# Two layer norms of the first tiles done by GpSimd in place of VectorE, in a fused attention and recurrent gate kernel

## Chip, cores and metric

One core of one Trainium2 chip. The metric is the device time of one execution in microseconds (us); lower is better.

## The reference

x is 8 x 512 x 512 (batch, position, feature), ctx_1024 of the same shape gives both keys and values.

```python
x = x + xattn(layernorm(x), ctx_1024, ctx_1024, W_proj, b_proj)
x = x + ffn(layernorm(x), ...)
```

`xattn` is attention with 16 heads of 32 features, in which a query sees the keys at most 64 positions away, then a projection with W_proj. `ffn` scans over the 8 batch entries with a 512 x 512 state c: ft and it are sigmoids and gt a tanh of xt @ w.T + c @ u.T + b, and c = ft * c + it * gt. The output is tanh(x @ wo.T + c_final @ uo.T + bo). The layer norm subtracts the mean of a row and multiplies by 1 / sqrt(var + 1e-5).

## The kernel before

The 4096 rows of x are 32 tiles of 128 rows; a tile has 4 slots, one for each group of 4 heads. A single list, `steps` (L114 to L330), holds all work in order, as pairs (kind, index). Each engine's program walks this same list and takes from it the kinds that are its own; so each engine works strictly in the list's order, and semaphores join the engines. n is the slot, i = n // 4 the tile, s = n % 4. The loop at L165 writes the list. Up to slot 19 ("early") a tile i does, in order: in s = 0 the projection ("proj", L806) of tile i-1, the copy of inverse sums ("recip", GpSimd L668), the query norm ("ln1b") of tile i+1, a pair of weight remainders ("rest", GpSimd L653), and the bias add ("bias", GpSimd L648) of tile i+1; in s = 1 the residual add ("resid", VectorE L1063) and the statistics ("stat2", with GpSimd's power at L673) of tile i-1, another "rest", the second norm ("ln2b", L1083) of tile i-1, and TensorE's transpose of the normed query rows ("query", L709); in s = 2 "turn2", TensorE's transpose of the second norm's output (L821), with ScalarE's rounding of it (L931) and VectorE's remainder (L1099), and in tiles 2 and 3 a third "rest"; in s = 3 the first statistics ("ln1", with GpSimd's power at L639) of tile i+2 and TensorE's "spread" of the inverse sums (L797), which waits for GpSimd's "recip". Each slot also has a "score" (L731, TensorE, then L1013, VectorE), "exp" (L901, ScalarE), "turn" (L743, L753) and "value" (L767, L774).

The pairs of L653 are spread by SPLIT_AT (L158): two in tile 1, three in tile 2, three in tile 3, two in tile 4. From slot 20 on the gates' matrix products ("cell", L684 to L686) fill TensorE between these steps, the projection follows the query norm in the list, and the pieces of attn_hi and attn_lo (L663) are made for it. SENT is 9 and TURNED_X 11: the query norm is a step of tiles 0 to 10 alone (later tiles load x already transposed and norm it in "query_norm"), while the second norm is a step of all 32 tiles.

One buffer, tile_row, holds in turn the normed query rows (xn), the attention output (attn) and the second norm's output (x2). So the query norm of tile i+1 waits for the projection of tile i-1, which reads attn (`projected`, up to tile 6), and for tiles 7 to 10 for the split of attn (`attn_split`, L663). The moments mv1 and mv2 and the inverse deviations rs1 and rs2 have two places each, used in turn. These are the lines of VectorE that normalise:

```python
dve.tensor_scalar(xn[:, :], xr[:, i % XR, :], mv1[:, r, 0:1], rs1[:, r:r + 1],
                  ALU.subtract, ALU.mult).then_inc(ln1, 1)
dve.tensor_scalar(x2[:, :], xr[:, i % XR, :], mv2[:, r, 0:1], rs2[:, r:r + 1],
                  ALU.subtract, ALU.mult).then_inc(x2_done, 1)
```

Of the kernel before, what the change touches and what calls it, by code (L numbers as in the profile page):

```python
# [7 lines left out]
ALU = mybir.AluOpType  # L8
# [12 lines left out]
def bass_xattn_ffn(nc, x, x_t, ctx_rows, ctx_t, w_proj, b_proj, w_gates, u_gates, biases, w_out, u_out, b_out, in_c,  # L21
# [41 lines left out]
    WHOLE = OWN_BANKS // G  # L63
# [3 lines left out]
    SENT = 2 * TT + 1  # L67
# [3 lines left out]
    TURNED_X = SENT + 2  # L71
    XR = 4
# [2 lines left out]


    MOVED = [j for j in range(SENT - 1, TILES) if j % TT < TT - 1]

    def moved(n):
        return sum(j < n for j in MOVED)  # L80

# [4 lines left out]
    def by_tensor(n):  # L86
        return n - moved(n)
# [77 lines left out]
    while cells_done < len(products):  # L165
        i, s = n // G, n % G
# [178 lines left out]
    with ExitStack() as ctx:  # L345
# [23 lines left out]
        xr = sb("xr", [P, XR, D], F32)  # L369
# [3 lines left out]
        xn = x2 = tile_row  # L373
# [26 lines left out]
        mv1 = invsum[:, MEAN:MEAN + 4].rearrange("p (r m) -> p r m", r=2)  # L400
        ve1, rs1 = invsum[:, MEAN + 4:MEAN + 6], invsum[:, RSTD:RSTD + 2]
# [11 lines left out]
        mv2 = moments[:, 0, :].rearrange("p (r m) -> p r m", r=2)  # L413
        ve2, rs2 = moments[:, 1, 0:2], moments[:, 1, 2:4]
# [23 lines left out]
        attn_split = sem("attn_split"); wp_lo = sem("wp_lo")  # L438
# [16 lines left out]
        q_turned = sem("q_turned"); scored = sem("scored"); turned = sem("turned"); turned_2 = sem("turned_2"); valued = sem("valued")  # L455
        spread = sem("spread"); projected = sem("projected"); state_used = sem("state_used")
        row_done = sem("row_done")
        x2_turned = sem("x2_turned"); gate_sum = sem("gate_sum")
# [30 lines left out]
        def need(eng, s, n):  # L489
            if n > 0:  # L490
                eng.wait_ge(s, n)
# [131 lines left out]
        @block.gpsimd  # L623
        def _(pool):
            pool.memset(ident[:, :], 0.0).then_inc(consts, 1)
            pool.memset(mask[:, :], 0.0).then_inc(consts, 1)
            pool.memset(half[:, :], -0.5).then_inc(consts, 1)
            pool.wait_ge(consts, 3)
            pool.affine_select(out=ident[:, :], in_=ident[:, :], compare_op=ALU.not_equal, fill=1.0,
                               base=0, pattern=[[-1, P]], channel_multiplier=1).then_inc(consts, 1)  # L630
            pool.affine_select(out=mask[:, :], in_=mask[:, :], compare_op=ALU.is_ge, fill=NEG,
                               base=-WINDOW, pattern=[[1, MASKW]], channel_multiplier=-1).then_inc(consts, 1)
            pool.wait_ge(consts, 5)
            pool.affine_select(out=mask[:, :], in_=mask[:, :], compare_op=ALU.is_ge, fill=NEG,
                               base=3 * WINDOW, pattern=[[-1, MASKW]], channel_multiplier=1).then_inc(consts, 1)
            for kind, i in steps:
                if kind == "ln1":
                    pool.wait_ge(var1, i + 1)
                    pool.tensor_tensor(rs1[:, i % 2:i % 2 + 1], ve1[:, i % 2:i % 2 + 1], half[:, :], ALU.pow)\  # L639
                        .then_inc(rstd1, 1)  # L640
                if kind == "bias":
                    if i < TURNED_X:
                        pool.wait_ge(ln1, i + 1)
                    else:
                        pool.wait_ge(stat1, i + 1)
                    if i == 0:
                        pool.wait_ge(bp_in, DMA)
                    pool.tensor_tensor(xr[:, i % XR, :], xr[:, i % XR, :], bp_row[:, :], ALU.add).then_inc(xr_ready, 1)  # L648
                if kind == "rest":
                    gt, u, k0 = chunks[i]  # L650
                    for k in range(k0, k0 + PAIR):
                        pool.wait_ge(w_hi, PAIR * i + k - k0 + 1)
                        pool.tensor_tensor(gate_w[:, gt, u, 1, k, :], raw_w[i % RAW][:, k - k0, :],  # L653
                                           gate_w[:, gt, u, 0, k, :].bitcast(F32), ALU.subtract).then_inc(w_lo, 1)
                if kind == "split_proj":
                    for k in range(i, i + PAIR):
                        pool.wait_ge(wp_hi, k + 1)
                        pool.tensor_tensor(proj_w[:, 1, k, :], wp[:, k, :], proj_w[:, 0, k, :].bitcast(F32),
                                           ALU.subtract).then_inc(wp_lo, 1)
                if kind == "halves":  # L660
                    pool.wait_ge(attn_round, i - WHOLE + 1)
                    need(pool, projected, i)
                    pool.tensor_tensor(attn_lo[:, :, :], attn if i < SENT else recip[:, :, :], attn_hi[:, :, :].bitcast(F32), ALU.subtract)\  # L663
                        .then_inc(attn_split, 1)
                if kind == "recip" and i < G * SENT:
                    pool.wait_ge(inverted, i + 1)
                    need(pool, spread, i // G)
                    pool.tensor_copy(recip[:, i % G, :].rearrange("p (h d) -> p h d", h=HPG),  # L668
                                     inv_rows[:, :, i % G].unsqueeze(2).to_broadcast([P, HPG, HEAD]))\
                        .then_inc(inv, 1)  # L670
                if kind == "stat2":
                    pool.wait_ge(var2, i + 1)
                    pool.tensor_tensor(rs2[:, i % 2:i % 2 + 1], ve2[:, i % 2:i % 2 + 1], half[:, :], ALU.pow)\  # L673
                        .then_inc(rstd2, 1)
            for o in range(len(outs) - 1):
                pool.wait_ge(tanhed, o + 1)
                pool.wait_ge(x1_in[o % X1_RING], DMA * (o // X1_RING + 1))
                row = h_ring[o % H_RING]
                pool.tensor_tensor(row, row, x1_ring[o % X1_RING], ALU.add).then_inc(summed, 1)
# [292 lines left out]
        def _(dve):  # L972
# [4 lines left out]
            for kind, i in steps:  # L977
                if kind == "ln1":
                    r = i % 2
                    dve.wait_ge(x_in[i % XR], DMA * (i // XR + 1))  # L980
                    dve.bn_stats(st1[:, r, :], xr[:, i % XR, :]).then_inc(stat1, 1)
                    dve.wait_ge(stat1, i + 1)
                    dve.bn_aggr(mv1[:, r, :], st1[:, r, :]).then_inc(aggr1, 1)
                    dve.wait_ge(aggr1, i + 1)
                    need(dve, rstd1, i - 1)
                    dve.tensor_scalar(ve1[:, r:r + 1], mv1[:, r, 1:2], EPS, None, ALU.add).then_inc(var1, 1)
                if kind == "ln1b":
                    r = i % 2
                    dve.wait_ge(rstd1, i + 1)
                    need(dve, q_turned, i)  # L990
                    if i > SENT:
                        dve.wait_ge(x2_turned, by_tensor(i - 2))
                    if i - 2 < WHOLE:
                        need(dve, projected, i - 1)
                    elif i <= SENT + 1:
                        dve.wait_ge(attn_split, i - 1 - WHOLE)
                    dve.tensor_scalar(xn[:, :], xr[:, i % XR, :], mv1[:, r, 0:1], rs1[:, r:r + 1],
                                      ALU.subtract, ALU.mult).then_inc(ln1, 1)
                if kind == "query_norm":
                    mean, rstd = [norm_rows[:, a, :].unsqueeze(1).to_broadcast([P, G, P]) for a in range(2)]  # L1000
                    dve.wait_ge(xt_in, DMA * (i - TURNED_X + 1))
# [15 lines left out]
                if kind == "recip":  # L1017
                    r, g = i // G % 2, i % G
# [45 lines left out]
                if kind == "stat2":  # L1064
                    r = i % 2
                    row = xr[:, i % XR, :]
                    dve.wait_ge(x1_done, i + 1)
                    dve.bn_stats(st2[:, r, :], row).then_inc(stat2, 1)
                    dve.wait_ge(stat2, i + 1)
                    dve.bn_aggr(mv2[:, r, :], st2[:, r, :]).then_inc(aggr2, 1)  # L1070
                    dve.wait_ge(aggr2, i + 1)
                    need(dve, rstd2, i - 1)
                    dve.tensor_scalar(ve2[:, r:r + 1], mv2[:, r, 1:2], EPS, None, ALU.add).then_inc(var2, 1)
                if kind == "ln2b":
                    r = i % 2
                    dve.wait_ge(rstd2, i + 1)
                    dve.wait_ge(q_turned, min(i + 3, TURNED_X))
                    need(dve, x2_turned, by_tensor(i))
                    if i + 2 >= TURNED_X:
                        dve.wait_ge(q_ready, min(i + 3, TILES))  # L1080
                    if i - 1 in MOVED:
                        dve.wait_ge(x2_lo, i)
                    dve.tensor_scalar(x2[:, :], xr[:, i % XR, :], mv2[:, r, 0:1], rs2[:, r:r + 1],  # L1083
                                      ALU.subtract, ALU.mult).then_inc(x2_done, 1)
# [144 lines left out]
```

## Time and profile before

| | |
|---|---|
| median of 3 runs | 943.76 us (943.57 to 945.68) |
| span of the profiled execution | 941.8 us |
| TensorE matmul, busy | 918.6 us, 98% |
| VectorE, busy | 676.1 us, 72% |
| ScalarE, busy | 476.5 us, 51% |
| GpSimd, busy | 204.8 us, 22% |
| granted TensorE clock | full in all 40 slices |

The profiled execution's own time outside its span isn't listed; the median of the runs is 2.0 us above the span. In the rows PE is TensorE's matmul side, DVE is VectorE, ACT is ScalarE, POOL is GpSimd. A busy time is the union of the instructions' durations; an idle time in square brackets stands in front of an instruction and names what ended it. Matmul ends are modelled.

### The profile page before, as it was taken

To read this page: it belongs to the slowest core of one execution; us is meant where nothing else is said; L and a number is where in the kernel's file an instruction comes from. 1 tells how busy PE (TensorE), PEld (TensorE's weight loads), DVE (VectorE), ACT (ScalarE), POOL (GpSimd) and SP (SyncE) were. 2 spreads that over 40 slices of the span, in tenths; PEclk is the share of its full clock that TensorE was granted. 3 is DMA by queue.
4 is the path that set the end of the run, shared out by engine and by line. 5 is a ranking of instruction groups with operands and counts; after the bars stand their busy time and mean duration, and the time that the engine had idled before them with its cause. 6 is when DMAs were issued, how large, how long until landed. Compare 5 with 4: busy or idle time off the path is not lost.

```text
span 941.8 us, 21981 instructions
## 1 busy us (share of the span) xinstructions
PE 918.6 (98%) x7842; PEld 715.5 (76%) x7842; DVE 676.1 (72%) x2281; ACT 476.5 (51%) x1430; POOL 204.8 (22%) x228
## 2 busy tenths in 40 slices
PE   7999999899999999999999999999999999999998
PEld 5555567678877788887887888788877888878887
DVE  6888898788779977998799878987798531143222
ACT  6888666655455544645565555555655321131222
POOL 5475322211101111111111111111101100003444
PEclk9999999999999999999999999999999999999999
DMA  9464232234444453544443444433333150059862
GB/s 305 161 192 150 88 96 69 87 89 126 135 111 134 119 143 96 135 110 124 130 141 112 121 114 122 115 107 110 97 98 91 50 163 0 1 179 382 307 237 101
DMA packets 139348, 123.58 MB, mean 131 GB/s; under 512 B 46824, under 2 KB 104168, under 8 KB 137704
## 3 DMA queue, kind: packets, MB, share of 16 engines
q1 hardware_dynamic: 138520, 121.91, 42.6%
q8 instruction: 63, 1.03, 0.5%
q10 hardware_dynamic: 720, 0.27, 0.2%
q14 instruction: 45, 0.37, 0.1%
HBM read 87.70 MB, written 34.46 MB: 130 GB/s over the span
## 4 chain that ended last, share of the span: by engine, by line
PE 85%; DVE 6%; issue 3%; ACT 2%; DMA 2%; POOL 1%; SPq 0%; DVEq 0%; ACTq 0%; POOLq 0%
PE ps_g L684 18%; PE ps_g L686 17%; PE ps_g L685 17%; PE ps_a L731 5%; PE ps_a L753 4%; PE ps_m L684 3%; PE ps_v L774 3%; PE ps_m L686 3%; PE ps_m L685 3%; PE ps_m L806 2%; PE ps_a L684 2%; PE ps_v L779 2%; DVE probs L1013 2%; PE ps_a L686 2%; PE ps_a L685 2%
## 5 line engine op out<-in xcount | busy, mean ns | idle before, releaser
L901 ACT ACTIVATE probs<-probs,rowmin 128x192 f32<-128x192 f32 (+1 forms) x512 | 239.4, 470 | 114.3 <-DVE rowmin L1013 114.3
L1013 DVE CUSTOM_DVE_ANT_0 probs<-ps_a,mask 128x192 f32<-128x192 f32 (+1 forms) x512 | 166.1, 386 | 31.7 <-PE ps_a L731 30.6
L684 PE MATMUL ps_g<-state_hi,gate_w 128*128 128x512 f32 x336 | 133.6, 398 | 0.0
L686 PE MATMUL ps_g<-state_hi,gate_w 128*128 128x512 f32 x336 | 131.1, 390 | 0.0
L685 PE MATMUL ps_g<-state_lo,gate_w 128*128 128x512 f32 x336 | 130.9, 389 | 0.0
L1048 DVE STREAM_TRANSPOSE keys<-probs 32x128 f32<-32x128 f32 x420 | 125.6, 299 | 5.2
L948 ACT ACTIVATE gate<-ps_g,bias 128x512 f32<-128x512 f32 x84 | 57.6, 686 | 105.7 <-PE ps_g L686 105.2
L901 ACT ACTIVATION_READ_ACCUMULATOR probs<-probs,rowmin 128x1 f32 x512 | 96.3, 188 | 0.0
L663 POOL TENSOR_TENSOR attn_lo<-recip,attn_hi 128x512 fp32r<-128x512 f32 x23 | 29.8, 1294 | 276.8 <-ACT attn_hi L914 276.8
L906 ACT ACTIVATE probs_t<-ps_a 128x512 f32<-128x512 f32 x108 | 59.3, 595 | 52.3 <-PE ps_a L753 52.3
L684 PE MATMUL ps_g<-x2t_even,gate_w 128*128 128x512 f32 x192 | 80.0, 417 | 0.0
L684 PE MATMUL ps_g<-x2t_odd,gate_w 128*128 128x512 f32 x192 | 76.9, 401 | 0.0
L686 PE MATMUL ps_g<-x2t_even,gate_w 128*128 128x512 f32 x192 | 75.2, 391 | 0.0
L685 PE MATMUL ps_g<-x2t_even,gate_w 128*128 128x512 f32 x192 | 75.0, 390 | 0.0
L686 PE MATMUL ps_g<-x2t_odd,gate_w 128*128 128x512 f32 x192 | 74.9, 390 | 0.0
L685 PE MATMUL ps_g<-x2t_odd,gate_w 128*128 128x512 f32 x192 | 74.8, 390 | 0.0
L686 PEld LDWEIGHTS ps_g<-state_hi,gate_w 128*128 128x128 f32 x336 | 63.1, 188 | 13.4
L684 PEld LDWEIGHTS ps_g<-state_hi,gate_w 128*128 128x128 f32 x336 | 63.1, 188 | 12.6
L685 PEld LDWEIGHTS ps_g<-state_lo,gate_w 128*128 128x128 f32 x336 | 63.2, 188 | 12.2
L731 PE MATMUL ps_a<-keys,queries 32*64 32x192 f32 (+1 forms) x2048 | 62.3, 324 | 4.6 <-DMA keys<-ctx_t 2.1
L753 PE MATMUL ps_a<-ident,probs 128*128 128x128 f32 x432 | 60.0, 274 | 1.2 <-ACT probs L901 0.6
L753 PEld LDWEIGHTS ps_a<-ident,probs 128*128 128x128 f32 x432 | 51.0, 139 | 12.4 <-ACT probs L901 3.6
(211 smaller groups left out, 1722.4 us busy)
## 6 DMA issues: line engine op xcount, KB each, us to landing
values<-ctx_rows SPq DMA_DIRECT2D x34, 256.0 KB, 4.3
xr<-x SPq DMA_DIRECT2D x32, 256.0 KB, 3.8
keys<-ctx_t SPq DMA_DIRECT2D x16, 512.0 KB, 4.2
x_dram<-xr SPq DMA_DIRECT2D x32, 256.0 KB, 2.6
gate_w<-x2t_dram SPq DMA_DIRECT2D x8, 1024.0 KB, 9.8
keys<-ctx_t SPq DMA_DIRECT2D x16, 384.0 KB, 3.4
x2t_dram<-x2t_even SPq DMA_DIRECT2D x12, 512.0 KB, 4.1
x2t_dram<-x2t_odd SPq DMA_DIRECT2D x12, 512.0 KB, 4.4
```

Of the source, the lines that this page charges most:

```text
L663: pool.tensor_tensor(attn_lo[:, :, :], attn if i < SENT else recip[:, :, :], attn_hi[:, :, :].bitcast(F32), ALU.subtract)\
L684: pe.matmul(ps, lhs[0], rhs[0], start=start, stop=False)
L685: pe.matmul(ps, lhs[0], rhs[1], start=False, stop=False)
L686: return pe.matmul(ps, lhs[1], rhs[0], start=False, stop=stop)
L731: mm = pe.matmul(ps_a[h][q, score_at[i] + k.start:score_at[i] + k.stop], queries[rows, g, q], keys[rows, key_home[tile], g, k], start=True ...
L753: mm = pe.transpose(ps_turn[i][:, h * P:(h + 1) * P], probs[:, i % 2, h, own:own + P], ident[:, :])
L774: pe.matmul(ps_v[HEAD * h:HEAD * (h + 1), g * P:(g + 1) * P], values[:, tile % 2, 0, d], own_home[i][:, h, :], start=True, stop=False)
L901: act.activation(row, row, ACT.Exp, bias=rowmin[:, i % 2, h:h + 1], scale=-1.0, accum_out=rowsum[:, i // G % 2, i % G, h:h + 1]).then_inc( ...
L906: act.activation(own_home[i], ps_turn[i][:, :].rearrange("p (a q) -> p a q", a=HPG), ACT.Copy)\
L948: act.activation(gate[:, min(gt, 1), :], ps_g[i % 2][:, :], ACT.Tanh, bias=(first_bias if b == 0 else bias)[:, gt, m:m + 1], scale=1.0 if ...
L1013: dve.tensor_tensor_reduce(probs[:, i % 2, h, 0:SEEN[t]], ps_a[h][:, score_at[i]:score_at[i] + SEEN[t]], mask[:, MASK0[t]:MASK0[t] + SEEN[ ...
L1048: turn = dve.transpose(side_home[i][BLK * keys_of:BLK * (keys_of + 1), :, q], probs[q, i % 2, :, col:col + BLK])
```

## The change

GpSimd takes "ln1b" (all its 11 tiles) and "ln2b" of tiles 0 to 7, with the same operation and the same waits, at the same places of the list. Two waits are added on VectorE, so that the statistics don't overwrite moments that GpSimd still reads.

```diff
+    POOL_NORMS = SENT - 1
...
@@ gpsimd
+                if kind == "ln1b":
+                    r = i % 2
+                    pool.wait_ge(rstd1, i + 1)
+                    need(pool, q_turned, i)
+                    if i > SENT:
+                        pool.wait_ge(x2_turned, by_tensor(i - 2))
+                    if i - 2 < WHOLE:
+                        need(pool, projected, i - 1)
+                    elif i <= SENT + 1:
+                        pool.wait_ge(attn_split, i - 1 - WHOLE)
+                    pool.tensor_scalar(xn[:, :], xr[:, i % XR, :], mv1[:, r, 0:1], rs1[:, r:r + 1],
+                                       ALU.subtract, ALU.mult).then_inc(ln1, 1)
+                if kind == "ln2b" and i < POOL_NORMS:
+                    r = i % 2
+                    pool.wait_ge(rstd2, i + 1)
+                    pool.wait_ge(q_turned, min(i + 3, TURNED_X))
+                    need(pool, x2_turned, by_tensor(i))
+                    pool.tensor_scalar(x2[:, :], xr[:, i % XR, :], mv2[:, r, 0:1], rs2[:, r:r + 1],
+                                       ALU.subtract, ALU.mult).then_inc(x2_done, 1)
...
@@ vector
                     dve.wait_ge(stat1, i + 1)
+                    need(dve, ln1, min(i - 1, TURNED_X))
                     dve.bn_aggr(mv1[:, r, :], st1[:, r, :]).then_inc(aggr1, 1)
...
-                if kind == "ln1b":
-                    r = i % 2
-                    dve.wait_ge(rstd1, i + 1)
-                    need(dve, q_turned, i)
-                    if i > SENT:
-                        dve.wait_ge(x2_turned, by_tensor(i - 2))
-                    if i - 2 < WHOLE:
-                        need(dve, projected, i - 1)
-                    elif i <= SENT + 1:
-                        dve.wait_ge(attn_split, i - 1 - WHOLE)
-                    dve.tensor_scalar(xn[:, :], xr[:, i % XR, :], mv1[:, r, 0:1], rs1[:, r:r + 1],
-                                      ALU.subtract, ALU.mult).then_inc(ln1, 1)
...
                     dve.wait_ge(stat2, i + 1)
+                    need(dve, x2_done, i - 1)
                     dve.bn_aggr(mv2[:, r, :], st2[:, r, :]).then_inc(aggr2, 1)
...
-                if kind == "ln2b":
+                if kind == "ln2b" and i >= POOL_NORMS:
```

## Rows read from the trace of the kernel before

**Rows 1.** The page's busy times, shares of the span and instructions.
```profile
PE 918.6 (98%) x7842; PEld 715.5 (76%) x7842; DVE 676.1 (72%) x2281; ACT 476.5 (51%) x1430; POOL 204.8 (22%) x228
```

**Rows 2.** By stretch: start:end, length, busy PE, PEld, DVE, ACT, POOL; clock, DMA.
```profile
0.00:100.00 100.00, 87.95 (x1026) 51.94 (x1027) 82.67 (x321) 76.51 (x242) 55.11 (x75) 1.00 0.61 191
100.00:200.00 100.00, 93.81 (x920) 67.87 (x926) 83.52 (x310) 64.96 (x198) 24.16 (x35) 1.00 0.31 93
```

**Rows 3.** TensorE's waits from 0 to 200 us: total us, times, longest.
```profile
PE ps_m L797 <- POOL recip L668: 2.3, 4, 1.2
PE ps_a L731 <- DMA keys<-ctx_t: 2.1, 2, 1.8
PE ps_a L731 <- DVE rowmin L1013: 1.9, 4, 0.7
PE ps_v L692 <- POOL ident L629: 1.9, 1, 1.9
```

**Rows 4.** Timeline of VectorE, norms alone: start us, duration us.
```profile
5.57 0.55 DVE L997 TENSOR_SCALAR tile_row<-xr,invsum 128x512 f32<-128x512 f32 x1 [0.67 <-POOL invsum L639]
...
63.12 1.07 DVE L997 TENSOR_SCALAR tile_row<-xr,invsum 128x512 f32<-128x512 f32 x1 [2.10 <-PE ps_m L806]
...
67.52 1.09 DVE L1083 TENSOR_SCALAR tile_row<-xr,moments 128x512 f32<-128x512 f32 x1
...
123.65 0.55 DVE L997 TENSOR_SCALAR tile_row<-xr,invsum 128x512 f32<-128x512 f32 x1
...
128.16 0.54 DVE L1083 TENSOR_SCALAR tile_row<-xr,moments 128x512 f32<-128x512 f32 x1
```

**Rows 5.** Timeline of GpSimd, in tile 3 and in tile 6 (last two rows).
```profile
61.41 2.51 POOL L653 TENSOR_TENSOR gate_w<-early_w,gate_w 128x512 fp32r<-128x512 f32 x2
64.27 1.28 POOL L648 TENSOR_TENSOR xr<-xr,bp_row 128x512 f32<-128x512 f32 x1 [0.36 <-DVE tile_row L997]
66.51 0.55 POOL L673 TENSOR_TENSOR moments<-moments,half 128x1 f32<-128x1 f32 x1 [0.96 <-DVE moments L1073]
67.03 2.71 POOL L653 TENSOR_TENSOR gate_w<-early_w,gate_w 128x512 fp32r<-128x512 f32 x2
...
121.91 0.29 POOL L668 COPY recip<-invsum 128x128 f32<-128x128 f32 x1 [2.59 <-DVE invsum L1024]
124.28 1.30 POOL L648 TENSOR_TENSOR xr<-xr,bp_row 128x512 f32<-128x512 f32 x1 [2.07 <-DVE tile_row L997]
```

**Rows 6.** Timeline of TensorE: projections, both norms' transposes, one spread.
```profile
25.46 3.67 PE L806 MATMUL ps_m<-state,tile_row 128*128 128x512 f32 x8
...
36.27 0.63 PE L821 MATMUL ps_m<-ident,tile_row 128*128 128x128 f32 x4 [0.23 <-DVE gate L1111]
...
43.11 3.67 PE L806 MATMUL ps_m<-state,tile_row 128*128 128x512 f32 x8 [0.17 <-DVE tile_row L1055]
...
52.54 0.66 PE L821 MATMUL ps_m<-ident,tile_row 128*128 128x128 f32 x4
56.61 0.66 PE L797 MATMUL ps_m<-ident,recip 128*128 128x128 f32 x4 [1.16 <-POOL recip L668]
59.28 3.70 PE L806 MATMUL ps_m<-state,tile_row 128*128 128x512 f32 x8
...
65.12 0.66 PE L709 MATMUL ps_m<-ident,tile_row 128*128 128x128 f32 x4
...
70.03 0.63 PE L821 MATMUL ps_m<-ident,tile_row 128*128 128x128 f32 x4
...
76.55 3.67 PE L806 MATMUL ps_m<-state,tile_row 128*128 128x512 f32 x8 [0.17 <-DVE tile_row L1055]
...
87.30 0.63 PE L821 MATMUL ps_m<-ident,tile_row 128*128 128x128 f32 x4
```

**Rows 7.** GpSimd's groups by form: mean duration and idle time before.
```profile
L631 POOL TENSOR_SCALAR_AFFINE_SELECT mask<-mask 128x384 f32<-128x384 f32 x1 | 0.5, 510 | 0.0
...
L629 POOL TENSOR_SCALAR_AFFINE_SELECT ident<-ident 128x128 f32<-128x128 f32 x1 | 0.3, 294 | 0.2 <-POOL half L627 0.2
```

## The prediction

> **What bounds the kernel now.** I read the page's busy times first, then those by stretch. TensorE is busy for 918.6 of the span's 941.8 us [rows 1], so it is idle for 23.2 us in all. Of these 12.05 us lie in the first 100 us and 6.19 us in the second [rows 2], which leaves 5 us for all the rest. So what this change can give or take lies in the first 200 us, and the budget for a gain is 18.2 us. There VectorE is busy 83 of 100 us and GpSimd 55, then 24 [rows 2]: the move looks natural by shares alone. Second, what TensorE waited for in that stretch [rows 3]: GpSimd's spreading of the inverse sums 2.3 us, a transfer of keys 2.1, VectorE's row minima 1.9, the identity at the start 1.9. No single wait is large, and TensorE hardly ever waited for the norms themselves. Third, the order of GpSimd's own work against TensorE's marks in each tile [rows 5, 6], which is where this change is decided. The span is 941.8 us; the median of the three runs is 2.0 us above it. I take these 2.0 us as fixed and add my sum to the median 943.76.
>
> **What leaves VectorE.** Eleven query norms (L997, for tiles 0 to 10) and eight second norms (L1083, tiles 0 to 7). Alone, the one takes 0.55 us and the other 0.54 [rows 4]. Nineteen times 0.545 is 10.4 us, and more in fact: the second norm at 67.52 took 1.09 us beside a pair of GpSimd subtractions that took 2.71 us, where the pair before it took 2.51 us alone [rows 4, 5]. So the two engines held each other up, by about 0.5 and 0.2 us. The Trainium skill (SBUF — State Buffer, on the shared port pair) says that a VectorE tensor_scalar in a two-port mode and a GpSimd instruction exclude each other for a whole instruction; by that rule, these collisions vanish with the change, and the rows fit it. VectorE also stops sitting in front of L997 until the projection ends (2.10 us idle before the one at 63.12 [rows 4]), but its next step, the residual add of the same tile, waits for the same projection. That wait moves; it isn't gained.
>
> **What GpSimd's norm costs.** The trace has no tensor_scalar on GpSimd. Lower end: its one-input affine_select takes 0.294 us for 128 columns and 0.510 for 384 [rows 7], so 0.84 ns for a column and 0.62 us for 512. Upper end: its two-input add of 512 columns, 1.28 us [rows 5]. The norm reads one tensor but does two arithmetic steps with two scalars per partition, so it is nearer to the lower; I take 0.75 us. The Trainium skill (GPSIMD Engine Reference, Performance versus the Vector engine) gives 769 ns for a tight loop over 512 elements and keeps elementwise work on VectorE as the rule; by its figure the four stalls below would be 6.1 us as an estimate, where mine come to 5.9.
>
> **The new chain on GpSimd, tiles 1 to 4.** GpSimd works its queue in order. In tile i's first slot that queue now holds: the query norm of tile i+1, which waits for the projection of tile i-1 because both share tile_row; a pair of weight subtractions ("rest", L653); the bias add (L648). In the second slot: the power (L673), another pair of L653, and only then the second norm of tile i-1. Before, the first pair ran while TensorE did the projection (61.41, within the projection at 59.28) [rows 5, 6]; now it is queued behind the wait. From the end of the projection to the end of the second norm: norm 0.75, pair 2.51, add 1.28, power 0.52 (66.51 to 67.03), pair 2.51, norm 0.75 and 0.2 for the two hand-overs, 8.52 us. TensorE used to reach the transpose of the second norm (L821) sooner [rows 6]:
> tile 1: 25.46 + 3.67 = 29.13 to 36.27, 7.14 us, so 1.4 late;
> tile 2: 46.78 to 52.54, 5.76 us, so 2.8 late, less the 1.16 us that TensorE waited for GpSimd at 56.61 in any case, 1.6;
> tile 3: 62.98 to 70.03, 7.05 us, 1.5 late;
> tile 4: 80.22 to 87.30, 7.08 us, 1.4 late.
> Together 5.9 us of new TensorE idle time. With the norm at 0.62 us it is 4.9, with 1.28 us 10.1 (two norms in each of four chains). Nothing covers it: the values, turns and scores of the next slots stand behind L821 in TensorE's order, and ScalarE's rounding and VectorE's remainder of the same tile come after it. TensorE's query transpose isn't hit: the norm would end near 63.9, and TensorE, after its turn and score, came to L709 at 65.12 [rows 6].
>
> **The start.** The first query norm is exposed: VectorE had waited 0.67 us for GpSimd's power before it, at 5.57 [rows 4]. On GpSimd it needs no hand-over but takes 0.2 us longer: +0.2 us, between 0 and 0.7.
>
> **Tiles 5 to 8.** The pairs of L653 are over, and the query norms of tiles 7 to 10 wait for GpSimd's own split of attn, no longer for the projection. After the copy at 121.91 GpSimd was idle for 2.07 us until VectorE had done this norm, at 123.65 [rows 4, 5]. So GpSimd does both norms here inside its idle time, and TensorE loses nothing: 0 us, and at most 0.5 for tile 6's norm, which still waits for the projection.
>
> **What VectorE's relief gives back.** About 1.1 to 2 us of VectorE work a tile. The waits it can shorten are the minima (1.9), the part of GpSimd's spreading not yet counted (2.3 less 1.16, 1.1) [rows 3], and smaller ones of VectorE's turned copies and products that I put at 2 to 3 from the idle total. That is some 5.5 us; while TensorE stands at L821 VectorE and ScalarE also catch up. I take half, 2.8 us. The lower end is 0, the upper the whole idle time less the start and the transfer, 18.2 - 1.9 - 2.1 = 14 us.
>
> **What else moves.** No DMA and no SyncE step moves, but loads of x wait for the second norm, at most 3 us later, three tiles ahead of their use: 0. The added VectorE waits, ahead of bn_aggr for the norm two tiles back, ask for something a whole tile old: 0; if GpSimd fell back by a tile, statistics, minima and copies would queue behind them. The weight remainders come up to 3 us later; the first cell needs them all, but the last pair ends at 80.22 + 0.75 + 2.51 + 1.28 + 0.52 + 2.51 = 87.8, and the first cell stands two slots behind the L821 at 87.30: 0.
>
> **Sum.** 5.9 + 0.2 - 2.8 = +3.3 us, 947.1 us. A difference of 0.3% (2.8 us) is about what a measurement of this kernel can tell from none, so I stand close to that edge.
>
> **Rivals.**
> (a) The forecast: GpSimd's order makes the second norm late, and the relief pays for half; +1 to +6 us. Chance 0.55.
> (b) The stalls are absorbed. ScalarE and VectorE are nearly as loaded as TensorE here, so TensorE's pause may only replace pauses further on: 5.9 against some 5.5, 943.8 to 944.5. For it: TensorE's waits are many and small [rows 3]; against it: TensorE is already 88% busy. 0.20.
> (c) Faster: VectorE's in-order queue is what sets the first 200 us, with its blocked stretch ahead of L997 the worst, and everything behind it moves up. If half of the 14 us goes and the chain costs 3, -4 us, 939.8. It decides if the norm takes 0.62 us or less and VectorE's chain comes out a microsecond a tile shorter. For it: 83% busy and 0.5 us lost in collisions; against it: even with 0.62 us the chain has 8.3 us against 7.1. 0.12.
> (d) GpSimd's norm is as slow as its adds, 1.28 us or more: 10.1 + 0.7 - 2.8 = +8, 951.8 us; then recip copies come late too and L797 waits. 0.13.
>
> **How the numbers follow.** Of (a) some 0.35 lies above 2.8 us, and all of (d): slower 0.50 with a little for (b)'s spread. Faster is most of (c), 0.11. The rest is 0.39. The range takes in the nearer part of (c) and reaches to (d)'s value, 942.0 to 952.0; what it leaves out, most of (c) and a slower (d), is 0.2 at most.
>
> **What would show it.** Right: the new GpSimd tensor_scalar near 0.75 us; a wait "PE ps_m L821 <- POOL tile_row" of 1 to 3 us, four times, between 35 and 95 us; TensorE idle time of the first 100 us up from 12 to 15 or 16, that of the second 100 us slightly down; VectorE's busy time down by 12 to 14 us; from 200 us on a plain shift. Wrong: no such wait (then the order isn't what decides), TensorE's idle time in the first 100 us not larger, or a norm above 1.2 us.

## The result, and the profile after

The changed kernel takes 970.23 us (970.07 to 970.31), against 943.66 us (942.75 to 945.68) for the kernel before on the same chip: a ratio of 1.0284, 95% interval 1.0271 to 1.0296, so 26.6 us slower where 3.3 us were forecast. The span is 968.1 us, 26.3 us more. First the page's busy times, then the busy times by stretch, in the columns of [rows 1] and [rows 2].

```profile
PE 929.2 (96%) x7842; PEld 722.0 (75%) x7842; DVE 663.9 (69%) x2262; ACT 476.9 (49%) x1430; POOL 242.5 (25%) x247
```

```profile
0.00:100.00 100.00, 78.18 (x818) 46.95 (x818) 58.33 (x244) 63.62 (x199) 59.57 (x70) 0.90 0.54 169
100.00:200.00 100.00, 89.03 (x904) 60.11 (x903) 72.41 (x285) 62.41 (x192) 50.34 (x52) 0.97 0.29 88
200.00:300.00 100.00, 99.14 (x912) 78.76 (x899) 80.67 (x285) 52.69 (x172) 18.54 (x19) 1.00 0.41 113
300.00:400.00 100.00, 98.93 (x914) 79.10 (x913) 85.07 (x289) 54.13 (x171) 15.83 (x16) 1.00 0.44 122
```

TensorE executes the same 7842 matmuls, but is busy with them for 10.6 us longer (929.2 against 918.6), and idle for 38.9 us where it was for 23.2, 15.7 us more. The two make up the 26.3 us. The idle time is 21.8 us in the first 100 us (12.05 before), where the forecast had 15 or 16, and 11.0 us in the second (6.19), where the forecast had slightly less than before: the later stalls have moved there. What was not forecast either is the column behind the busy times: TensorE's granted clock is 0.90 and 0.97 on average in these stretches, where it was 1.00 throughout.

TensorE's waits from 0 to 200 us, to set beside [rows 3]:

```profile
PE ps_m L842 <- POOL tile_row L660: 19.5, 5, 5.6
PE ps_m L730 <- POOL tile_row L653: 4.0, 4, 2.2
PE ps_v L713 <- POOL ident L631: 1.9, 1, 1.9
```

L842 is the transpose of the second norm (L821 before), L730 that of the query norm (L709 before). The wait that the prediction named is there, five times instead of four and up to 5.6 us long, instead of 1 to 3. Why it is so long is in GpSimd's group of the query norms (count, total us, mean ns) and in its timeline in tile 2, beside [rows 5]:

```profile
L653 POOL TENSOR_SCALAR tile_row<-xr,invsum 128x512 f32<-128x512 f32 x11 | 22.9, 2079 | 10.0 <-PE ps_m L827 9.7 <-POOL attn_lo L684 0.2
```

```profile
55.28 2.08 POOL L653 TENSOR_SCALAR tile_row<-xr,invsum 128x512 f32<-128x512 f32 x1 [1.61 <-PE ps_m L827]
57.32 2.52 POOL L674 TENSOR_TENSOR gate_w<-early_w,gate_w 128x512 fp32r<-128x512 f32 x2
59.80 1.27 POOL L669 TENSOR_TENSOR xr<-xr,bp_row 128x512 f32<-128x512 f32 x1
61.02 0.56 POOL L694 TENSOR_TENSOR moments<-moments,half 128x1 f32<-128x1 f32 x1
61.55 2.49 POOL L674 TENSOR_TENSOR gate_w<-early_w,gate_w 128x512 fp32r<-128x512 f32 x2
64.01 2.08 POOL L660 TENSOR_SCALAR tile_row<-xr,moments 128x512 f32<-128x512 f32 x1
```

The order is the one that the prediction worked out, link by link; but a norm takes GpSimd 2.08 us, not 0.75, and more than the 1.28 us that I had set as the upper bound. From TensorE's timeline, beside [rows 6]:

```profile
7.79 1.11 PE L730 MATMUL ps_m<-ident,tile_row 128*128 128x128 f32 x4 [2.21 <-POOL tile_row L653]
...
28.56 3.67 PE L827 MATMUL ps_m<-state,tile_row 128*128 128x512 f32 x8
...
43.39 1.12 PE L842 MATMUL ps_m<-ident,tile_row 128*128 128x128 f32 x4 [3.99 <-POOL tile_row L660]
...
51.40 3.67 PE L827 MATMUL ps_m<-state,tile_row 128*128 128x512 f32 x8 [0.17 <-DVE tile_row L1065]
...
66.15 1.11 PE L842 MATMUL ps_m<-ident,tile_row 128*128 128x128 f32 x4 [5.62 <-POOL tile_row L660]
...
135.22 0.66 PE L842 MATMUL ps_m<-ident,tile_row 128*128 128x128 f32 x4 [1.99 <-POOL tile_row L660]
```

From the end of the projection to L842 are 43.39 - 32.23 = 11.16 us in tile 1 and 66.15 - 55.07 = 11.08 us in tile 2. The prediction's sum with 2.08 in place of 0.75 is 6.82 + 2 x 2.08 + 0.2 = 11.18. L842's own four transposes took 1.11 and 1.12 us in these two tiles, where L821 took 0.63 to 0.66 [rows 6]. Stretches of 2 us around the second stall show the reason:

```profile
60.00:62.00 2.00, 0.53 (x16) 0.21 (x16) 1.69 (x9) 1.82 (x8) 2.00 (x3) 1.00 0.95 331
62.00:64.00 2.00, 0.00 (x0) 0.00 (x0) 0.00 (x0) 0.00 (x0) 2.00 (x2) 0.51 0.67 239
64.00:66.00 2.00, 0.00 (x0) 0.00 (x0) 0.00 (x0) 0.00 (x0) 2.00 (x2) 0.50 0.00 0
...
70.00:72.00 2.00, 2.00 (x21) 1.05 (x20) 1.71 (x5) 1.71 (x8) 0.01 (x1) 0.50 0.98 246
72.00:74.00 2.00, 2.00 (x41) 1.52 (x40) 1.94 (x11) 1.22 (x3) 0.84 (x2) 0.93 1.03 329
```

While TensorE stands idle, its granted clock falls from 1.00 to 0.50 (2.4 to 1.2 GHz); the work resumes at 66.15 and runs at the lower level until 72. Between 62 and 66 us GpSimd is the only compute engine at work: TensorE, VectorE and ScalarE all stand.

The loss is complete early. L842 comes 7.1, 13.6, 19.0, 24.1 and 27.7 us later than L821 did in tiles 1 to 5, and in tiles 6, 7 and 8 it is 27.7 us late again. From there on nothing is added; the span ends 26.3 us later.

### The profile page after: what moved, and what is told of

It reads as the page before. It is cut to its first block, busy times and chain, and to the rows that moved or that the text cites. A ratio compares the mean times of both kernels' runs of the same rounds, so it can differ in the third digit from the quotient of the medians.

```text
span 968.1 us, 22041 instructions
## 1 busy us (share of the span) xinstructions
PE 929.2 (96%) x7842; PEld 722.0 (75%) x7842; DVE 663.9 (69%) x2262; ACT 476.9 (49%) x1430; POOL 242.5 (25%) x247
## 4 chain that ended last, share of the span: by engine, by line
PE 84%; POOL 5%; DVE 4%; issue 3%; ACT 2%; DMA 1%; SPq 0%; POOLq 0%; DVEq 0%; ACTq 0%
PE ps_g L705 17%; PE ps_g L707 17%; PE ps_g L706 17%; PE ps_a L752 5%; PE ps_a L774 4%; PE ps_m L705 3%; PE ps_v L795 3%; PE ps_m L707 3%; PE ps_m L706 3%; PE ps_m L827 2%; PE ps_a L705 2%; PE ps_v L800 2%; PE ps_a L706 2%; PE ps_a L707 2%; POOL gate_w L674 1%
## 5 line engine op out<-in xcount | busy, mean ns | idle before, releaser
L705 PEld LDWEIGHTS ps_g<-state_hi,gate_w 128*128 128x128 f32 x336 | 63.1, 188 | 12.7
L706 PEld LDWEIGHTS ps_g<-state_lo,gate_w 128*128 128x128 f32 x336 | 63.2, 188 | 12.2
```

The costliest lines, as they stand in the source:

```text
L705: pe.matmul(ps, lhs[0], rhs[0], start=start, stop=False)
L706: pe.matmul(ps, lhs[0], rhs[1], start=False, stop=False)
```

## The experiments

### One half of the change at a time

Query norms alone on GpSimd:

```diff
-    POOL_NORMS = SENT - 1
+    POOL_NORMS = 0
```

> Only the query norms (tiles 0 to 10) are on GpSimd; all second norms are back on VectorE. Theory (GpSimd's order with a norm of 2.08 us): from the end of a projection to TensorE's transpose of the second norm now stand norm 2.08, pair 2.5, add 1.25, power 0.5, VectorE's norm 0.6 to 1.1, in all some 7.5 us against 7.1 before, so 0.4 us late in tiles 1, 3 and 4; tile 2 is late by some 2 us through its third pair and the copies; the start costs 1.5 for tile 0's norm and 1.3 for tile 1's. Sum +5 to +9 us, 949 to 953, with no stretch of lowered clock between 36 and 120 us. Rival (each norm on GpSimd costs alike, whatever stands around it): 11 of 19 norms, so 11/19 of 26.6, +15 us, 959.

Measured: 960.03 us against 942.88, +17.2 us (ratio 1.0182, 1.0167 to 1.0197). The theory's +5 to +9 missed; the rival's +15 came close, but its reason, a like cost for each norm, doesn't hold: the late norms are free, as a run below shows. From three timelines of tile 1, VectorE, GpSimd, TensorE:

```profile
39.24 1.49 DVE L1094 TENSOR_SCALAR tile_row<-xr,moments 128x512 f32<-128x512 f32 x1 [1.85 <-POOL moments L694]
40.65 0.17 DVE L1034 RECIPROCAL invsum<-rowsum 128x4 f32<-128x4 f32 x1
40.74 1.24 DVE L1122 STREAM_TRANSPOSE gate<-ps_m 32x128 f32<-32x128 f32 x4
```

```profile
38.64 0.56 POOL L694 TENSOR_TENSOR moments<-moments,half 128x1 f32<-128x1 f32 x1
39.18 2.67 POOL L674 TENSOR_TENSOR gate_w<-early_w,gate_w 128x512 fp32r<-128x512 f32 x2
```

```profile
42.12 0.63 PE L842 MATMUL ps_m<-ident,tile_row 128*128 128x128 f32 x4 [2.33 <-DVE gate L1122]
```

I had left out who stands behind a wait. GpSimd's power (L694) comes late, behind the query norm, a pair and the bias add. VectorE then stands for 1.85 us in front of its own second norm, meets the running pair (1.49 us instead of 0.55), and only then turns the column that TensorE needs to have gone from ps_m before L842. The clock, expected to stay full from 36 to 120 us, was down too, to 0.95 in each of the first two stretches of 100 us.

Second norms alone on GpSimd (VectorE's "ln1b" put back, GpSimd's taken out):

```diff
@@ gpsimd
-                if kind == "ln1b":
...
@@ vector
+                if kind == "ln1b":
...
```

> Only the second norms of tiles 0 to 7 are on GpSimd; all query norms are back on VectorE. Theory (order): the first pair again runs during the projection, so the second norm ends 0.5 + 2.5 + 2.08 us after its statistics, 1.6 us late in tiles 1, 3 and 4, some 2 to 3 us late in tile 2, 1 us late in tile 5; less 1 to 2 us of relief: +6 to +9 us, 950 to 953. No TensorE wait for it is over 3 us, and the clock stays full. Rival (each norm costs alike): 8/19 of 26.6, +11 us, 955. If theory holds, the two halves sum to some 14 us, and 12 of the 26.6 us come only with both, as queue time added up past the point where TensorE's clock falls.

Measured: 952.36 us against 942.88, +9.5 us (1.0106, 1.0088 to 1.0125), a little over the theory's +6 to +9 and under the rival's +11. TensorE's largest wait is again for the second norm, 9.2 us in five, the longest 2.9. The clock was not quite full, 0.98 in the first 100 us. The two halves sum to 26.7 us, the whole is 26.6, so my expectation that 12 us come only from both together was wrong. That the sums agree doesn't show that the halves work independently: with the query norms alone VectorE was the late engine, which it isn't in the changed kernel. Divided by all norms, free ones included, a query norm costs 1.56 us and a second norm 1.19.

### What the instruction costs, and what decides it

A small kernel of its own, eight forms of instruction on one engine after the other:

```python
tensor_scalar(o[:, :], row[:, :], mean, scale, ALU.subtract, ALU.mult)        # L30
tensor_scalar(o[:, 0:256], row[:, 0:256], mean, scale, ALU.subtract, ALU.mult) # L31
tensor_scalar(o[:, :], row[:, :], 0.25, 1.5, ALU.subtract, ALU.mult)          # L32
tensor_scalar(o[:, :], row[:, :], mean, None, ALU.subtract)                   # L33
tensor_scalar(o[:, :], row[:, :], 1.5, None, ALU.mult)                        # L34
tensor_tensor(o[:, :], row[:, :], other[:, :], ALU.subtract)                  # L35
tensor_tensor(o[:, :], row[:, :], mean.to_broadcast([P, D]), ALU.subtract)    # L36
tensor_copy(o[:, :], row[:, :])                                               # L37
```

> No part of the reference is computed: one tile is put through eight forms of elementwise instruction, three times each, first on GpSimd and then on VectorE, each waiting for the one before (the rest of the output is a copy of x). Forms: tensor_scalar with two per-partition scalars on 512 and on 256 columns, with two constants, with one per-partition scalar, with one constant; tensor_tensor; tensor_tensor with a broadcast column; copy. Theory A (the two arithmetic steps cost): two-step forms near 2.08 us on GpSimd, one-step forms near 1. Theory B (the per-partition scalars cost): the form with constants near 1, forms with a per-partition scalar near 2. Theory C (GpSimd's tensor_scalar is slow in all forms): all near 2, with tensor_tensor at 1.28 and the copy near 0.6. VectorE: 0.4 to 0.55 us for the tensor_scalars on 512 columns, 0.6 to 0.7 for tensor_tensor.

Its groups, costliest first: count, then busy us and mean ns of one.

```profile
L30 POOL TENSOR_SCALAR pooled<-row,other 128x512 f32<-128x512 f32 x3 | 6.2, 2072 | 3.9 <-DMA other<-x 3.7
L32 POOL TENSOR_SCALAR pooled<-row 128x512 f32<-128x512 f32 x3 | 5.8, 1922 | 0.3
L33 POOL TENSOR_SCALAR pooled<-row 128x512 f32<-128x512 f32 x3 | 4.7, 1560 | 0.3
L34 POOL TENSOR_SCALAR pooled<-row 128x512 f32<-128x512 f32 x3 | 4.5, 1489 | 0.3
L35 POOL TENSOR_TENSOR pooled<-row,other 128x512 f32<-128x512 f32 x3 | 3.8, 1262 | 0.2
L31 POOL TENSOR_SCALAR pooled<-row,other 128x256 f32<-128x256 f32 x3 | 3.7, 1218 | 0.3
L36 POOL TENSOR_TENSOR pooled<-row 128x512 f32<-128x512 f32 x3 | 3.1, 1038 | 0.2
...
L37 POOL COPY pooled<-row 128x512 f32<-128x512 f32 x3 | 1.8, 612 | 0.2
L30 DVE TENSOR_SCALAR vectored<-row,other 128x512 f32<-128x512 f32 x3 | 1.6, 546 | 39.8 <-POOL pooled L37 39.7
```

Theory C is the nearest, though its "all near 2" holds for the two-step forms alone: GpSimd's tensor_scalar is slow in every form, 1.49 us for one step with a constant, where a subtraction of two whole tensors takes 1.26. The second step adds 0.43 to 0.51 us, per-partition scalars 0.07 to 0.15. From 256 to 512 columns it goes by 3.3 ns a column. Reading one tensor is thus no mark of a cheap instruction here: the copy reads one and takes 0.61 us, the norm reads one and takes 2.07. VectorE takes 0.546 us for the same norm, 3.8 times less.

### The same change with a shorter norm

The changed kernel, with GpSimd's norms on the first columns only; the other columns of the norms are left out, so the time is that of the same order with a cheaper instruction. A memset of tile_row (0.5 us) is added at GpSimd's start, and the first norm waits for it.

```diff
-                    pool.tensor_scalar(xn[:, :], xr[:, i % XR, :], mv1[:, r, 0:1], rs1[:, r:r + 1],
+                    pool.tensor_scalar(xn[:, 0:96], xr[:, i % XR, 0:96], mv1[:, r, 0:1], rs1[:, r:r + 1],
...
-                    pool.tensor_scalar(x2[:, :], xr[:, i % XR, :], mv2[:, r, 0:1], rs2[:, r:r + 1],
+                    pool.tensor_scalar(x2[:, 0:96], xr[:, i % XR, 0:96], mv2[:, r, 0:1], rs2[:, r:r + 1],
```

> The changed kernel, but GpSimd's 19 norms cover 96 of the 512 columns only (0.42 + 96 x 0.0033 = 0.74 us by the two widths measured, which is the duration that the prediction took; the other columns keep what the buffer held). Theory (the working was right and the instruction's duration was the mistake): the prediction's own sum holds, 945 to 949 us, TensorE waits 1 to 2 us for the second norm in tiles 1 to 4, and its clock stays full. Rival (the queue or the relief was misjudged too): 952 or more, with waits elsewhere, or 942 or less.

Measured: 948.56 us against 943.61, +5.0 us (1.0054, 1.0039 to 1.0069), with 0.69 us a norm. TensorE's waits from 0 to 200 us:

```profile
PE ps_m L845 <- POOL tile_row L663: 7.0, 4, 2.9
```

Four waits of 7.0 us in all, the longest 2.9, where 5.9 were worked out. The time is inside the stated 945 to 949, but not all for the stated reason, so the agreement is in part luck. Its page, of an execution of 949.70 us, has TensorE busy for 923.6 us, 5.0 more than before, and idle for 24.2, only 1.0 more. So in idle time the new waits were nearly all made good elsewhere, and nearly all of the loss shows as slower matmuls: the clock, which I had said would stay full, was 0.95 in the first 100 us. A slower TensorE also waits less for the others, so the two parts can't be told apart cleanly.

The same with 256 columns:

> The same with 256 of the 512 columns, 1.22 us each, close to the price of the prediction's rival (d). [...] Rival (cost is linear in the norm's duration, 26.6 us for 1.53 us over VectorE's 0.55): 0.74 gives 3.3 us, 1.22 gives 11.6 us, 955.

Measured: 956.33 us, +12.7 us (1.0141, 1.0124 to 1.0158), with 1.23 us a norm. My theory, the prediction's sum with this norm (10.1 + 0.7 - 2.8 = +8 us), had 949 to 954 us and a loss that grows faster for longer norms. The linear rival (955) came closer. Over norms of 0.69, 1.23 and 2.08 us the loss is 5.0, 12.7 and 26.6 us, about 14 and 16 us for each microsecond of the norm: no clear bend. In the three profiles TensorE's extra busy time is 5.0, 8.1 and 10.6 us, its extra idle time 1.0, 7.0 and 15.7: the slower clock is there with the shortest norm already, the waiting grows later. (The two narrow profiles are of the slowest of their four executions, 949.70 and 958.81 us, so their parts are 1 to 2.5 us too large in sum.)

### TensorE's clock

Idle work for TensorE before its wait for the second norm; the transposes are read by nothing.

```diff
                 if kind == "turn2" and i not in MOVED:
-                    pe.wait_ge(x2_done, i + 1)
                     need(pe, q_ready, min(i + 3, TURNED_X))
                     need(pe, column_turned, len([n for n in row_at if n < G * (i + 1) + 2]))
+                    for _ in range({0: 26, 1: 38, 2: 26, 3: 26, 4: 12}.get(i, 0)):
+                        pe.transpose(ps_m[:, 0:P], ident[:, :], ident[:, :])
+                    pe.wait_ge(x2_done, i + 1)
```

> The changed kernel, with idle work for TensorE (26, 38, 26, 26 and 12 transposes of the identity into ps_m, which nothing reads) just before it waits for the second norm of tiles 0 to 4. Theory (the 26.6 us are 15.7 us of TensorE idle time and 10.6 us of the same matmuls running slower): the stalls stay as long in time, the clock stays full from 36 to 120 us, and the time falls by about 10 us, to 958 to 962. Rival (the lowered clock is a mark of the stall and costs nothing by itself, since other engines would be waited for anyway): 968 to 971.

Measured: 963.41 us, 6.8 us less than the changed kernel; the theory's range ended at 962. The clock is 1.00 from 40 us on, but 0.91 from 20 to 40, where the changed kernel's own profile has 1.00 with the same start. The start was filled as well, 16 and 9 transposes ahead of `pe.wait_ge(ln1, i + 1)` for tiles 0 and 1:

> The kernel with the filled waits (e3_filled), and besides 16 and 9 transposes of the identity before TensorE waits for the query norms of tiles 0 and 1. Theory: the lowered clock of the stretch from 20 to 40 us follows the idle time of the start and vanishes, which gives back another 1 to 2 us: 961 to 962.5. The rest over the kernel before, some 18 us, is waiting. Rival (that stretch's clock has another cause): 963.5, with the clock lowered there again.

Measured: 961.04 us (1.0181, 1.0162 to 1.0201). The stretches up to 60 us, in the columns of [rows 2]:

```profile
0.00:20.00 20.00, 15.82 (x187) 11.89 (x191) 10.85 (x51) 10.23 (x33) 11.20 (x20) 1.00 0.94 292
20.00:40.00 20.00, 18.63 (x218) 11.03 (x219) 15.35 (x61) 16.44 (x53) 14.96 (x16) 1.00 0.58 190
40.00:60.00 20.00, 18.13 (x215) 12.19 (x214) 12.35 (x52) 14.86 (x45) 11.52 (x13) 1.00 0.46 136
```

The clock is full throughout and 9.2 of the 26.6 us are back (8.5, if each kernel is set against the runs of the kernel before beside it), though none of the kernel's own instructions was changed. The lowered clock is thus a cost of its own. What is left, 18.0 us over the kernel before, is the waiting: TensorE is idle for 23.3 us, as before the change (23.2), and busy for 935.6, 17.0 us more, with the idle transposes that fill the new waits.

Some 1.5 us of this gain lie in the start, where the granted clock doesn't show them: it reads 1.00 from 5 to 15 us in the changed kernel's profile, yet the first query transposes (7.79) took 1.11 us, where before the change they took 0.66 at 6.17, and the four groups of matmuls behind them were as slow. With the start filled they take 0.66 again. TensorE before the change, and with only the late norms moved (a run below), where the same wait is followed by slow transposes:

```profile
6.17 0.66 PE L709 MATMUL ps_m<-ident,tile_row 128*128 128x128 f32 x4 [0.73 <-DVE tile_row L997]
```

```profile
6.20 1.12 PE L730 MATMUL ps_m<-ident,tile_row 128*128 128x128 f32 x4 [0.61 <-DVE tile_row L1019]
```

The Trainium skill (TensorE: Matmul & The Clock Gate, Part 1) says that an idle TensorE falls to 1.2 GHz and comes back to 2.4 GHz only after it has been busy for a while; the changed kernel's stretches from 60 to 74 us agree. The waits alone don't tell when it falls, though. With the query norms of tiles 0 and 1 back on VectorE (a run below), it fell to 0.65 behind waits of 0.4 and 1.2 us that the changed kernel passes at full clock:

```profile
144.00:148.00 4.00, 3.84 (x25) 2.97 (x26) 3.76 (x17) 0.71 (x3) 1.54 (x2) 0.65 0.00 0
```

What decides it stays open here.

### GpSimd's order, and the start

The changed kernel with the pairs elsewhere in the list:

```diff
-            steps.extend(("rest", c) for c in SPLIT_AT.get(n - 1, [])[1:2])
...
             tile_steps("ln2b", i - 1)
+            if early:
+                steps.extend(("rest", c) for c in SPLIT_AT.get(n - 1, [])[1:2])
...
         if s == 0:
+            steps.extend(("rest", c) for c in SPLIT_AT.get(n, [])[0:1])
             tile_steps("ln1b", i + 1)
-            steps.extend(("rest", c) for c in SPLIT_AT.get(n, [])[0:1])
```

> The changed kernel with all norms on GpSimd at full width, but two pairs of weight remainders per tile stand elsewhere in GpSimd's list: the first pair before the query norm (it runs during the projection again), the second behind the second norm. Theory (order): between projection and second transpose stand two norms, the bias add and the power, 6.1 us, or 8.6 where the first pair overruns the projection, so the 4 us waits of tiles 1, 3 and 4 fall to 0 to 1.5 and the clock stays full there; tiles 2 and 3 wait about 1.5 us at the spread for the copies behind the pairs; the start (3 us) and tiles 5 and 6 stay. 949 to 956 us. Rival (GpSimd is simply too slow, wherever the pairs stand): 964 or more.

Measured: 956.67 us against 943.61, +13.1 us (1.0137, 1.012 to 1.0154), 0.7 us over the theory's range and far from the rival's 964. Half of the loss goes by order alone, with the same 19 norms of 2.08 us. TensorE's waits, 0 to 200 us:

```profile
PE ps_m L731 <- POOL tile_row L654: 6.0, 5, 2.2
PE ps_m L819 <- POOL recip L690: 5.4, 4, 2.6
PE ps_m L843 <- POOL tile_row L661: 3.3, 2, 2.0
```

The wait for the second norm (L843 here) fell from 19.5 to 3.3 us; part of it moved to the query norm (L731, 4.0 us in the changed kernel), which an overrunning first pair makes late, and to the copies (L819) behind the pairs. GpSimd is now in the path at three places.

The changed kernel with the query norms of tiles 0 and 1 back on VectorE (`kind == "ln1b" and i >= 2` on GpSimd, `i < 2` on VectorE):

> The changed kernel, with the query norms of tiles 0 and 1 given back to VectorE; the other 17 norms stay on GpSimd. Theory: the first projection had begun 3.1 us later than before the change (28.56 against 25.46), all of it from those two norms, and this comes back: 966 to 968 us. Rival (what is lost at the start is made good later, since the later tiles are bound by GpSimd's chain and not by the start): 969 to 971.

Measured: 968.20 us (1.0257, 1.0237 to 1.0277), at the edge of what was expected: 2.0 of the 3.1 us of head start last. The stalls behind are no longer than they were (L842 waits 19.5 us in five again), and in tile 5 L842 is still 3.2 us ahead (132.04 against 135.22). Then 1.6 us go in one stretch, the one at a clock of 0.65 shown above: its projection takes 4.4 us, where it takes 2.9 in the changed kernel.

### Where the move is free, and a try for a faster kernel

GpSimd does only the query norms of tiles 7 to 10 and the second norms of tiles 5 to 7:

```diff
@@ gpsimd
+                if kind == "ln1b" and i >= WHOLE + 2:
...
+                if kind == "ln2b" and WHOLE <= i < POOL_NORMS:
...
@@ vector
+                if kind == "ln1b" and i < WHOLE + 2:
...
+                if kind == "ln2b" and not WHOLE <= i < POOL_NORMS:
```

> GpSimd does only the query norms of tiles 7 to 10 and the second norms of tiles 5 to 7, where its queue holds no pairs of weight remainders; the rest is on VectorE as before. Theory: 2.08 us fit into GpSimd's idle time, VectorE is relieved of 7 x 0.55 us, TensorE waits for none of it: 942 to 944 us, no difference that can be measured. Rival (2 us in place of 0.55 lie on the path anywhere): 7 x 1.5, 953.

Measured: 942.82 us against 943.61, ratio 0.9993 (0.9984 to 1.0003): no difference. Its norms take the same 2.08 us, and no wait of TensorE for them is among its longest. So the duration alone does no harm where GpSimd has the time.

The kernel before, with the second pair behind the copy ("recip") of its slot and the third pair behind that of the next:

```diff
-            steps.extend(("rest", c) for c in SPLIT_AT.get(n - 1, [])[1:2])
...
-        if s == 2:
-            steps.extend(("rest", c) for c in SPLIT_AT.get(n - 2, [])[2:3])
         if n + 1 < SLOTS:
             steps.append(("recip", n + 1))
...
+        if s == 1 and early:
+            steps.extend(("rest", c) for c in SPLIT_AT.get(n - 1, [])[1:2])
+        if s == 2:
+            steps.extend(("rest", c) for c in SPLIT_AT.get(n - 2, [])[2:3])
```

> The kernel before, all norms on VectorE; GpSimd's second and third pair of weight remainders stand behind the copy of the inverse sums of their slot and no longer ahead of it. Theory: the second norm no longer meets a running pair (0.5 us each, four times, not all on the path) and TensorE's 1.2 us wait for the copies in tile 2 goes: 941.5 to 943 us, -0.5 to -2 against the runs beside it. Rival (nothing of this is on the path): no change.

Measured: 943.51 us against 943.01, ratio of 0.9995 (0.9984 to 1.0007). And with both:

> The same order, and GpSimd does the query norms of tiles 7 to 10 and the second norms of tiles 5 to 7, as in e7_late_only. Theory: the two gains add up, 941 to 942.5 us, -1 to -2.5 against the runs beside it. Rival (the second gain, 0.8 us without certainty, was noise): as e13_before_pairs_late.

Measured: 942.77 us, ratio 0.9989 (0.9977 to 1.0001). Both are above the expected 941.5 to 943 and 941 to 942.5 us. TensorE's wait for the copies did fall, from 2.3 us [rows 3] to 1.5 in both, but none of the three kernels is told apart from the kernel before. No version that is surely faster was found.

## Why the prediction was wrong

The sign and the wait were right, the size was not: +26.6 us against +3.3, and outside the range, whose upper end was 952.0. With the measured norm in it, the forecast's own sum gives 5.9 + 8 x 1.33 = 16.5 us of stalls and 1.5 for the start, less 2.8: +15.3. So the norm's price accounts for 12.0 of the 23.3 us that are missing; the lowered clock (9.2) and tile 5 (2.0), both left out, make up nearly all of the rest. By its steps:

**What GpSimd's norm costs: the step that failed.** "I take 0.75 us", between 0.62 from affine_select and 1.28 from the two-input add. It is 2.08 us. The upper end was no bound: I took a two-input instruction as dearer than any with one input, and the forms run shows the reverse. It enters twice per tile. The figure of 769 ns from the Trainium skill (GPSIMD Engine Reference), for a tight loop and set beside mine, is as far from what this instruction takes.

**The chain, tiles 1 to 4: right.** With 2.08 us its own sum gives 11.18 us, and 11.16 and 11.08 were measured. The stalls are 4.0, 4.2 (11.08 - 5.76 - 1.16), 4.1 and 4.0 us against 1.4 to 1.6 forecast, 16.3 us in all for 5.9. The narrow norm of 0.69 us shows the same from the other side: 7.0 us of these waits, and a time 1.5 us above the forecast.

**The start: +0.2 forecast.** TensorE reached the first projection at 28.56 instead of 25.46 us, 3.1 late: 1.6 from the longer first norm (its transpose began at 7.79 us, before the change at 6.17), and 1.5 from the matmuls at about half speed behind it, since with the start filled the projection begins at 27.08. This second part isn't surely the change's doing: the run with late norms alone, whose start is that of the kernel before, has the same slow transposes (1.12 us at 6.20). Tile 1's wait (L730, 1.3 us), which I had not looked at, is made up before the projection. Giving both norms back gained 2.0 us.

**Tiles 5 to 8: partly right.** The query norms of tiles 7 to 10 cost nothing. The second norm of tile 4 costs 2 us, the fifth wait at L842: in tile 5 GpSimd's list has a pair of projection remainders (L679, 2.54 us) where the tiles before have L674, which I had overlooked.

```profile
130.56 2.54 POOL L679 TENSOR_TENSOR proj_w<-state,proj_w 128x512 fp32r<-128x512 f32 x2
133.09 2.07 POOL L660 TENSOR_SCALAR tile_row<-xr,moments 128x512 f32<-128x512 f32 x1
```

The run with late norms alone shows the others to be free.

**The lowered clock: left out.** No term of the sum and no rival held it, and it costs 9.2 us by the filled runs. The rows before couldn't show it: TensorE's longest wait there was 1.9 us, and the clock was full in every stretch.

**VectorE's relief: not measured by itself.** The terms are 16.3 for the chain, 1.6 for the start's longer norm, 2.0 for tile 5 and 9.2 for the clock, which holds the start's other 1.5: 29.1 us. The result is 26.6; the 2.5 us between them are near the 2.8 that I took for the relief, but they are a remainder, with the error of every term in it. In the narrow run waits of 7.0 us left only 1.0 us of new idle time, which points to more.

**What stands behind a wait: incomplete.** I had followed the norm to its reader, but not the late power (L694) to VectorE's second norm. With the query norms alone this made VectorE's queue the late one, and that half costs 17.2 us of the 26.7.

Rival (d), the slow norm, had the right mechanism at 0.13 but was priced with the same wrong upper end. Rival (c) is refuted: VectorE's busy time fell by 12.2 us, as forecast, and TensorE's waits grew. Rival (b), that stalls are absorbed, holds for part of them only.

## What to carry to other kernels

A step moved to an engine with idle time carries the wait that it holds into that engine's queue: add up everything that stands in the queue between that wait and the next thing that others need, with the new engine's duration at each place, and do the same for each result that comes late. Where the trace has never seen an operation on an engine, its nearest relative is no upper bound; measure the very form first, since a kernel with a few instructions is enough. And price a stall of TensorE by more than its length: here some 9 us for the same matmuls at the lower clock came on top of some 18 us of waiting.

## What the runs showed that I had not expected

GpSimd does a tensor_scalar of 512 columns with two steps in 2.07 us, but a tensor_tensor with a broadcast column in 1.04 us: with one step, that form beats tensor_scalar (1.56 us), and two of them would take as long as the single instruction that does both.

TensorE's clock fell even in the run with norms of 0.69 us, whose longest wait for a norm was 2.9 us; the mean of its first 100 us is 0.95.

Work that is thrown away made the changed kernel faster: 153 transposes of the identity, all put where TensorE had to wait, gave 9.2 us.

The granted clock is not the whole record of TensorE's speed: in the changed kernel's first 15 us it reads 1.00 while transposes take 1.11 instead of 0.66 us.
